# A four-layer stack on one core: one expert tile fewer, a reordered routing stage and added clock-keeping products

## What is computed

```python
def _L1_ffn_ref(x, rw1, rw2, w1, b1, w2, b2):      # 8 experts, 256 -> 1024 -> 256
    logits = _gelu(x @ rw1) @ rw2
    probs = jax.nn.softmax(logits, axis=-1)
    wgt, idx = jax.lax.top_k(probs, 2)
    for e in range(E):
        Ye = _gelu(x @ w1[e] + b1[e]) @ w2[e] + b2[e]
        Ce = _gelu(b1[e]) @ w2[e] + b2[e]
        for k in range(2):
            mask = idx[..., k] == e
            active = jnp.any(mask).astype(x.dtype)
            term = jnp.where(mask[..., None], Ye, Ce)
            out = out + active * wgt[..., k:k + 1] * term
```

## Time and profile before

| | |
|---|---|
| median of 3 runs | 454.55 us (454.42 to 456.42) |
| the profiled execution | 456.11 us, span 454.3 us |
| busy: PE, DVE, ACT, POOL | 387.2, 343.7, 294.3, 93.0 us |
| the chain that ended last, by engine | PE 58%, DVE 23%, ACT 8%, issue 9% |
| granted clock of PE, mean | 0.931 |

### The profile page before, as it was taken

The page is one execution under the profiler, slowest core; times in us unless marked ns, Lnnn a source line. Parts: engine busy times, 40 slices in busy tenths (PEclk is TensorE's granted clock), DMA queues, the critical chain, the costliest instruction groups (busy, mean ns, idle before and its releaser), DMA issues.

```text
span 454.3 us, 7376 instructions
## 1 busy us (share of the span) xinstructions
PE 387.2 (85%) x2617; PEld 336.5 (74%) x2628; DVE 343.7 (76%) x512; ACT 294.3 (65%) x518; POOL 93.0 (20%) x103
## 2 busy tenths in 40 slices
PE   3999665699883489999999999999999988898866
PEld 3998643477762379999999999999995876777523
DVE  5999969789465999999999913980014587989995
ACT  5996784478885277675766767676542555776754
POOL 3000002000030142332536322456430000000000
PEclk9999869699896589999999999999998899999989
DMA  7600000000057615711161486550006000000001
GB/s 286 203 1 1 2 0 0 0 1 1 0 185 272 207 47 181 248 49 35 36 221 37 156 282 234 161 209 27 14 23 198 0 1 0 2 12 25 1 25 35
DMA packets 22757, 38.82 MB, mean 85 GB/s; under 512 B 2089, under 2 KB 17082, under 8 KB 22594
## 3 DMA queue, kind: packets, MB, share of 16 engines
q1 hardware_dynamic: 17634, 25.50, 16.9%
q0 software_dynamic: 2624, 7.34, 4.9%
q10 hardware_dynamic: 2464, 5.51, 3.3%
HBM read 33.10 MB, written 5.24 MB: 84 GB/s over the span
## 4 chain that ended last, share of the span: by engine, by line
PE 58%; DVE 23%; issue 9%; ACT 8%; DMA 1%; POOL 1%; POOLq 0%; SPq 0%; ACTq 0%; DVEq 0%
PE bank L1559 19%; PE bank L1538 18%; PE bank L1398 3%; PE bank L1369 2%; PE bank L1429 2%; DVE scr L830 2%; DVE scr L832 2%; PE bank L1620 2%; PE bank L1530 1%; PE bank L1610 1%; PE bank L1416 1%; PE bank L1587 1%; DMA v<-in_kT 1%; POOL small L368 1%; DVE big L1196 1%
## 5 line engine op out<-in xcount | busy, mean ns | idle before, releaser
L1538 PE MATMUL bank<-big,yT 128*128 x384 | 86.7, 379 | 0.0
L611 ACT ACTIVATE yT<-bank,big 128x128 f32<-128x128 f32 x192 | 54.7, 368 | 46.9 <-PE bank L1559 46.8
L1538 PEld LDWEIGHTS bank<-big,yT 128*128 128x128 f32 x384 | 71.2, 190 | 8.7
L401 POOL DMA_INDIRECT xg<-token_rows,rowi x24 | 37.1, 1545 | 60.2 <-PE bank L1530 35.7
L368 POOL TENSOR_TENSOR small<-small 128x2 f32<-128x2 f32 (+1 forms) x9 | 10.1, 1117 | 191.3 <-DVE small L1216 85.7
L416 POOL DMA_INDIRECT choice_rows<-yo,rowo x24 | 28.2, 1174 | 64.2 <-ACT yo L620 48.8
L1369 PE MATMUL bank<-identf,scr 128*128 128x128 f32 x240 | 31.5, 292 | 3.8 <-DVE scr L843 3.8
L1369 PEld LDWEIGHTS bank<-identf,scr 128*128 128x128 f32 x240 | 30.7, 209 | 4.1 <-DVE scr L843 4.0
L1559 PEld LDWEIGHTS bank<-ygT,w3T 128*128 128x128 f32 x256 | 30.8, 198 | 1.0 <-issue 0.6
L1559 PEld LDWEIGHTS bank<-ygT,big 128*128 128x128 f32 x256 | 29.8, 192 | 1.9 <-issue 1.6
L1559 PE MATMUL bank<-ygT,big 128*128 128x128 f32 x256 | 29.9, 275 | 1.4 <-ACT ygT L603 1.4
(11 more groups left out here) (353 smaller groups left out, 831.3 us busy)
## 6 DMA issues: line engine op xcount, KB each, us to landing
big<-in_moe_w SPq DMA_DIRECT2D x16, 1024.0 KB
v<-in_kT SPq DMA_DIRECT2D x2, 512.0 KB, 4.5
big<-in_gateT SPq DMA_DIRECT2D x1, 1024.0 KB, 7.0
big<-in_upT SPq DMA_DIRECT2D x1, 1024.0 KB, 9.0
big<-in_downT SPq DMA_DIRECT2D x1, 1024.0 KB, 11.5
x<-in_x_bsc SPq DMA_DIRECT2D x1, 1024.0 KB, 13.8
token_rows<-y POOLq DMA_DIRECT2D x4, 256.0 KB, 7.4
ek<-in_w3a ACTq DMA_DIRECT2D x1, 1024.0 KB
```

The costliest lines, as they stand in the source:

```text
L401: gp.indirect_dma_start(out=xg[:, j % 3], out_offset=None, in_=Y1, in_offset=bass.IndirectOffsetOnAxis(ap=rowi[:, j:j + 1], axis=0)).then_ ...
L611: ins = sc.activation(hT[j % 2][:, c], ps[1 + 2 * (j % 2) + c // 4][:, (c % 4) * P:(c % 4 + 1) * P], ACT.Gelu, bias=b1s[:, c, j:j + 1])
L1538: ins = te.matmul(ps[5 + 2 * (j % 2)][:, 0:C], hT[j % 2][:, c], big[:, bass.ds(at + (W2_AT + c * C), C)], start=(c == 0), stop=(c == IC - 1))
```

## The change

The last expert's constant row no longer takes a slot. So its count is rounded up without it, and 23 tiles always suffice. Its constant is made apart: ACT takes Gelu of the last expert's `b1` (a 24th column of the turned `b1`), DVE sums the eight blocks of `w2` times this per partition into `last_w2`, PE sums over the partitions, ACT copies the row, SP puts it into `cb`.

The masks come from running counts: a scan over the experts of each token counts the candidates that reach the maximum, and the first is where the count is 1. The first mask is taken from the shifted logits, ahead of the exponential; the softmax is divided out behind the masks, and the two weights (`top`) are made after the tables. `rowi` is written ahead of `table`.

Eight calls of `keep_clock` are added, one is taken away, and the lengths of three others changed; the bias products are spread among them.

```diff
-    TILES = (2 * NT + E) // P + E
+    TILES = 2 * NT // P + E - 1
...
+            sp.wait_ge(s["last_row"], 1)
+            sp.dma_start(cb[E - 1:E, :], last_w2[E - 1:E, :]).then_inc(s["ld_cb"], 16)
...
             copy_w1(1)
+            sc.activation(last_g[:], b1s[:, :, TILES], ACT.Gelu).then_inc(s["last_gelu"], 1)
...
+            act.wait_ge(s["last_ps"], 1)
+            sc.activation(last_w2[0:E, :], ps[6][0:E, 0:C], ACT.Copy).then_inc(s["last_row"], 1)
             store_yo(TILES - 1)
...
+            def first_of(k):
+                link(ve.tensor_tensor_scan(count, fresh, cand_row, 0.0, ALU.mult, ALU.add))
+                link(ve.scalar_tensor_tensor(mask[:, :, k], tmp64, 1.0, cand, ALU.is_equal, ALU.mult))
+
+            dve.wait_ge(s["lg_shift"], 1)
+            link(ve.tensor_scalar(cand, lg, 0.0, None, ALU.is_equal))
+            first_of(0)
             dve.wait_ge(s["lg_exp"], 1)
+            link(ve.scalar_tensor_tensor(rest, mask[:, :, 0], -2.0, pr, ALU.mult, ALU.add))
+            link(ve.tensor_reduce(rmax, rest, AX.X, ALU.max))
+            link(ve.tensor_tensor(cand, rest, rmax.unsqueeze(2).to_broadcast([P, T, E]), ALU.is_equal))
+            first_of(1)
...
+            link(ve.tensor_tensor(both, mask, slot.rearrange("p (e t) -> p t e", t=T).unsqueeze(2).to_broadcast([P, T, 2, E]), ALU.mult))
+            link(ve.tensor_reduce(posf.rearrange("p k t -> p t k"), both, AX.X, ALU.add))
...
+            dve.wait_ge(s["last_gelu"], 1)
+            dve.wait_ge(s["ld_w"], 32 * E)
+            for c in range(IC):
+                at = (E - 1) % RING * EW + W2_AT + c * C
+                if c == 0:
+                    ins = ve.tensor_scalar(last_w2[:], big[:, at:at + C], last_g[:, c:c + 1], None, ALU.mult)
+                else:
+                    link(ins)
+                    ins = ve.scalar_tensor_tensor(last_w2[:], big[:, at:at + C], last_g[:, c:c + 1], last_w2[:], ALU.mult, ALU.add)
+            ins.then_inc(s["last_sum"], 1)
...
             te.matmul(ps[7][:, 0:2 * T * E], onesf[:], small[:, 320:448], start=True, stop=True).then_inc(s["cum_ready"], 1)
+            keep_clock(4, 14)
...
                 pe.wait_ge(s["a_ready"], n // T + 1)
+                if n == T:
+                    keep_clock(4, 2)
...
+            keep_clock(4, 9)
             pe.wait_ge(s["table_ready"], 1)
...
-            keep_clock(3, 3)
+            keep_clock(3, 4)
             x_transpose(0)
-            keep_clock(3, 2)
+            keep_clock(3, 1)
...
+            pe.wait_ge(s["last_sum"], 1)
+            te.matmul(ps[6][0:E, 0:C], last_e[:, 0], last_w2[:], start=True, stop=True).then_inc(s["last_ps"], 1)
             down_tile(TILES - 1, before)
...
             def down_l2(p, t):
+                if p >= 1 and t == 0:
+                    pe.wait_ge(s["x_l2"], p)
+                    keep_clock(3, 6)
                 pe.wait_ge(s["h2_ready"], HP2 * (p + 1))
-                if p >= 1:
-                    pe.wait_ge(s["x_l2"], p)
...
                 elif p >= 2:
+                    if p == G:
+                        keep_clock(0, 9)
                     turn_l3(2 * p - 3)
```

More of the change, by code:

```diff
@@ L174, in bass_adaln_ffn_stack @@
         gc = small[:, 656:784].rearrange("p (t m e) -> p t m e", t=T, m=2)
+        rest = cond[:].rearrange("p b d -> p (b d)")[:, 0:T * E].rearrange("p (t e) -> p t e", t=T)
+        both = cond[:].rearrange("p b d -> p (b d)")[:, 64:64 + 2 * T * E].rearrange("p (t k e) -> p t k e", t=T, k=2)
         tmp64 = small[:, 784:848].rearrange("p (t e) -> p t e", t=T)
         rt = sb("rt", [P, 6, T * E])
-        msum, incl, offs, slot, reset, ctiles = (rt[:, i] for i in range(6))
+        msum, incl, offs, slot, reset, fresh = (rt[:, i] for i in range(6))
         posf = small[:, 96:112].rearrange("p (k t) -> p k t", k=2)
@@ L189, in bass_adaln_ffn_stack @@
         row_c = sb("row_c", [P, 3, TILES])
-        of_tile = sb("of_tile", [P, TILES])
+        of_tile = sb("of_tile", [P, TILES + 1])
+        last_e = sb("last_e", [P, 3, E])
+        last_w2 = sb("last_w2", [P, C])
+        last_g = sb("last_g", [P, IC])
         nti = small[:, 72:80]
@@ L194, in bass_adaln_ffn_stack @@
         iota_t = sb("iota_t", [P, TILES])
-        tcmp = sb("tcmp", [P, TILES, E])
+        tcmp_all = sb("tcmp", [P, 24, E])
+        tcmp = tcmp_all[:, 0:TILES]
         ex3 = small[:, 864:1120].rearrange("p (k n) -> p k n", k=4)
-        ex_w = [ex3, tcmp[:].rearrange("p t e -> p (t e)").rearrange("p (k n) -> p k n", k=3)]
+        ex_w = [ex3, tcmp_all[:].rearrange("p t e -> p (t e)").rearrange("p (k n) -> p k n", k=3)]
         te_ = sb("te_", [P, 3, TILES])
@@ L335, in _ @@
             gp.memset(reset, 1.0)
+            gp.memset(fresh, 1.0)
             gp.memset(identf[:], 0.0)
@@ L597, in _ @@
             act.wait_ge(s["b1_turned"], 1)
-            sc.activation(b1s, ps[5][:, 0:IC * TILES].rearrange("p (c j) -> p c j", c=IC), ACT.Copy).then_inc(s["b1s_ready"], 1)
+            sc.activation(b1s, ps[5][:, 0:IC * (TILES + 1)].rearrange("p (c j) -> p c j", c=IC), ACT.Copy).then_inc(s["b1s_ready"], 1)
             def copy_xT(j):
@@ L1114, in _ @@
             gate, coef = gc[:, :, 1], gc[:, :, 0]
+            link(ve.tensor_tensor(both, mask, pr.unsqueeze(2).to_broadcast([P, T, 2, E]), ALU.mult))
+            link(ve.tensor_reduce(top.rearrange("p k t -> p t k"), both, AX.X, ALU.add))
             ve.tensor_tensor(gate, mask[:, :, 0], top[:, 0].unsqueeze(2).to_broadcast([P, T, E]), ALU.mult)
@@ L1683, in down_last @@
                 te.matmul(ps[7][:, 0:C], pick[:], br[:, H3:H3 + C], start=False, stop=True).then_inc(s["d3_ready"], 1)
-            for p in range(G):
-                bias(p)
+            bias(0)
+            keep_clock(6, 4)
+            bias(1)
+            keep_clock(6, 4)
             x_to_channels(0)
+            keep_clock(6, 2)
+            bias(2)
+            bias(3)
             pe.wait_ge(s["l2_int"], 1)
-            keep_clock(6, 9)
             for p in range(G + 2):
```

74 lines of the change are left out of this document (33 added, 41 removed).

## The result

| | before | changed |
|---|---|---|
| median | 455.18 us (4 runs, 454.42 to 456.42) | 442.7 us (4 runs, 441.51 to 444.43) |
| the profiled execution | 456.11 us, span 454.3 | 443.32 us, span 441.5 |
| busy: PE, DVE, ACT, POOL | 387.2, 343.7, 294.3, 93.0 us | 385.7, 351.2, 289.9, 92.1 us |
| granted clock of PE, mean | 0.931 | 0.959 |

The ratio is 0.9724 (95% interval 0.9702 to 0.9747): faster. The forecast was 440.2, its range 438.2 to 445.2.

The account below looks back on a forecast made before the run. PE was taken to bound the expert loop at 7.245 us a tile, full clock. Terms summed to -14.4 us, taking the profiled 456.11 to 441.7; less 1.56 to the median, the forecast was 440.2 us, range 438.2 to 445.2.

Parts of the forecast that it names:

- The tile: Expert loop: 24 passes become 23, saving one tile distance, -7.25 us.
- The `last_w2` product: PE's one fp32 product of 256 columns ahead of the last tile's down product: an eighth of a down product, +0.45 us.
- rival E: Slower than before: PE waits for DVE's `last_sum` ahead of the last down product; 457 us if 31 us late; chance 0.02.
- Routing: Logits to tile 0: shorter DVE chains, row numbers ahead of tables, ACT's chain last; tile 0 starts 2.5 us earlier.
- The bounds: -3.5, if tile 0 also runs at full clock: Limits on the routing term of -2.5 us: -3.5 with tile 0 at full clock, +0.7 if dummies don't restore the clock.
- Rival A: Routing dummies don't bring the clock back; tile 0 +0.7 us instead of -2.5, 443.4 us in all; chance 0.13.
- Layer-2 start: Bias products split by dummies, x transposed sooner, gate-up earlier and at full clock: -2.75 us.
- rival B: The clock falls in the layer-2 start all the same; +2 us there instead of -2.75, 445.0 us; chance 0.14.
- Pairs: Six dummies ahead of the down product of pairs 1 to 3: pair 2 saves 1.7 us, pair 3 pays 0.35.
- rival C: The clock falls in the two gaps in spite of the dummies; 2.9 us less gained, 443.1 us; chance 0.08.
- Tail: End of layer 3: nine dummies in PE's 2.70 us wait keep the clock, so DVE no longer waits for ACT: -1.2 us.

Follow-up runs that it names:

- The experiment: The change without the six dummies ahead of layer 2's down products and the nine at the end of layer 3: 448.97 us, ratio 0.9847.
- the best version: The change with the Gelu table loaded earlier, third weight load held until the first gather landed, three tail dummies instead of eight: 439.35 us, ratio 0.9644.

## Why the prediction was right, and where not

- *The tile*: right, 7.24 us against 7.245. *The `last_w2` product*: +0.73 us instead of +0.45. It was sized as an eighth of a down product; it is two instructions, 0.60 us long, with its own weight load. DVE's eight products took 8.2 us, not 4, still covered. Five of the last seven take 0.48 us, as forecast; the other two, 2.79 and 1.42 us, and the first of all, 1.34, run while POOL computes (L403 from 306.29 to 308.90, and a cast each beside the other two). In the run with 24 tiles, where POOL had no such work at that time, all eight took 4.0 us. The forecast had no such term; rival E is excluded, since DVE then idles 17.47 us.
- *Routing*: masks -1.84 measured from the logits (forecast -1.65), second `in_slot` -2.49 (-2.4), row numbers -3.67 (-3.4), tables -1.77 (-1.6), tile 0 -2.51 (-2.5). The reason was half wrong: I had the gather landing at 156.1 by adding the old interval, and ACT alone last. It landed at 156.7, behind the weight load, level with ACT. That tile 0 comes out on the forecast is in part luck: the tables were 0.17 us better than forecast, and ACT then waited 0.25 for the transposes. Nor is "rows ahead of tables" a part of the gain in the change as it stands: put back, it costs nothing.
- **The step that failed**: "The bounds: -3.5, if tile 0 also runs at full clock". I looked only for a better clock than before, and took the old length of tile 0 as the worse end. The four dummies were to end near 155.8 and the gather to land at 156.1, a gap of 0.3 us; they ended at 155.4 and it landed at 156.7, and the clock, just won back, fell again and stayed low for most of tile 0. +1.19 us. The missing term is a tile 0 slower than before; by the runs its size is sound, while the pause is only one candidate for what brings the fall about.
- *Rival A* is refuted as it was put: the b1 products ran at full clock. Its premise, that everything hangs on these dummies, is too: without them the change is no slower (441.82 us).
- *Layer-2 start*: -2.38 instead of -2.75, clock 1.00 throughout, so rival B did not happen. The two bias groups with their eight dummies took 4.1 us, not 3.6, and two dummies with the other two groups 2.4, not 2.1; so PE and not DVE set when gate and up began.
- *Pairs*: -1.51 between pairs 2 and 3, -1.35 forecast. Both gaps held the clock, rival C did not happen. The experiment shows that the dummies there protect about 4 us in its profile rather than the 2.9 that I gave rival C.
- *Tail*: -0.65 instead of -1.2. DVE's last block did start 1.18 us earlier, measured from the wait, as forecast; the eight old dummies, for which DVE's lateness had been cover, then gave 0.5 back. I named no cover for them.

The misses on the profiled execution add up to +1.6 us. The other 0.9 of the gap to 442.7 is the step to the median: I took 1.56 off as for the kernel before, and the change's median lies only 0.6 below its profiled execution. Most of this is chance in few executions: with a fourth one the median before is 455.18, only 0.93 below its profiled execution.

## What to carry to other kernels

Dummy products pay only if the clock that they hold is still there when the work on the path begins; here it fell just ahead of tile 0, and what 25 dummies had bought was gone. Five more in the last wait kept it. So look at the granted clock where the work starts, fill the last wait first, and size the filler by the measured landing, not by the wait before the change. When an upstream wait goes, look through everything downstream that it had covered: eight old dummies turned from free to 0.5 us. And before a row number or an index is hurried to a gather, look at what the DMA engines carry at that time.

## What the runs showed of the hardware

- In the change the gather's queue moved nothing in the windows up to 155, until a bulk load issued 3.8 us before it was nearly through; the gather took 4.6 us behind the load and 3.4 with the load held back.
- A wait of about 2 us lost the clock in one profile and not in another: in the kernel before only pair 2's (2.01 us, pair 1's was 2.04), without the gap dummies pair 1's (2.15) and pair 2's (2.11). One profile can't price such a wait.
- With four dummies ahead of the first transposes the clock fell at 154.1 in the run with the third load later, with pauses of at most 0.16 us since the b1 products, and in the best version, the same but for ACT's table load and the tail, it held.
- After a table load ACT went on within 0.01 us (154.52 + 1.28, then 155.81), where its input was there.
- DVE's product of a 128x256 block with a scalar per partition, added to an accumulator, took 0.48 us, but 2.79 beside POOL's product of 2.61 us that had started 0.10 us before it, and 1.42 beside a cast on POOL. The mean of the seven, 0.98, hides this.
